# Perceiver block on one core: the latent projection one slot later, its z stores on ScalarE's queue, x1 stores and raw weight loads at the end of the stage

## The reference

```
x  = x + softmax(layernorm(x) @ ctx^T / sqrt(512), masked) @ ctx        # ctx: 256 rows per batch element
h  = layernorm(x)
q  = rmsnorm(h @ wq_a^T + b) @ wq_b^T + b ; kv, k_pe = split(h @ wkv_a^T + b) ; kv = rmsnorm(kv)
x  = x + causal latent attention (16 heads, rotary part of 64) @ wo^T + b
x  = layernorm(relu(x @ up)^2 @ down + (x @ expert) * top-2 gate sum) * gamma + beta
```

## Time and profile before

| | us |
|---|---|
| median of 3 runs | 1123.19 |
| lowest, highest | 1122.73, 1124.93 |
| the profiled execution | 1125.78 |
| its span | 1124.0 |
| PE busy in the span | 1093.4 (97%) |
| DVE, ACT, POOL busy | 532.3, 351.8, 322.5 |
| stage x and the seam end at about | 182 |

### The profile page before, as it was taken

How to read it: one execution, slowest core, us unless ns; L and a number is a source line. 1 busy time by engine, 2 the same in 40 slices (tenths; PEclk the granted TensorE clock), 3 DMA queues, 4 the chain that set the end, 5 groups by cost and what they waited for, 6 DMA issues and landing times.

```text
span 1124.0 us, 20917 instructions
## 1 busy us (share of the span) xinstructions
PE 1093.4 (97%) x8097; PEld 950.2 (85%) x8097; DVE 532.3 (47%) x998; ACT 351.8 (31%) x699; POOL 322.5 (29%) x370
## 2 busy tenths in 40 slices
PE   5999999999999999999999999999999999999996
PEld 2676686888888888888888888889899998989895
DVE  3565565534443444344443456746244443525242
ACT  4456554332322222222322225513121221213130
POOL 2343361121212111121112122525242332415151
PEclk9999999999999999999999999999999999999998
DMA  9999922002111111102111117401010010101000
GB/s 363 417 421 418 422 96 72 22 20 73 28 33 56 42 56 33 56 19 61 32 38 56 39 51 232 169 1 39 1 38 20 20 38 0 37 0 38 1 19 19
DMA packets 41279, 100.96 MB, mean 90 GB/s; under 512 B 7497, under 2 KB 11620, under 8 KB 36740
## 3 DMA queue, kind: packets, MB, share of 16 engines
q1 hardware_dynamic: 41220, 100.16, 24.8%
HBM read 74.45 MB, written 17.30 MB: 82 GB/s over the span
## 4 chain that ended last, share of the span: by engine, by line
PE 91%; DVE 2%; DMA 2%; issue 2%; POOL 1%; ACT 1%; SPq 1%; DVEq 0%; POOLq 0%
PE b_z L44 7%; PE b_z L45 6%; PE b_z L46 6%; PE b_score L44 5%; PE b_score L45 5%; PE b_score L46 5%; PE b_prob L44 5%; PE b_prob L46 5%; PE b_prob L45 5%; PE b_z L1095 3%; PE b_read L44 3%; PE b_free L44 2%; PE b_read L46 2%; PE b_read L45 2%; PE b_free L46 2%; PE b_free L45 2%
## 5 line engine op out<-in xcount | busy, mean ns | idle before, releaser
L811 POOL TENSOR_TENSOR m_e<-m_e,m_rs 128x512 f32<-128x512 f32 x32 | 34.7, 1085 | 357.3 <-DVE m_rs L966 357.3
L1441 POOL TENSOR_TENSOR f_hT_lo<-f_h,f_hT_hi 128x512 fp32r<-128x512 f32 x64 | 89.6, 1399 | 94.0 <-ACT f_hT_hi L1484 89.3
L46 PE MATMUL b_z<-m_zT_hi,m_wq_hi 128*128 128x256 f32 x384 | 108.7, 283 | 0.0
L44 PE MATMUL b_z<-m_zT_lo,m_wq_hi 128*128 128x256 f32 x384 | 108.7, 283 | 0.0
L45 PE MATMUL b_z<-m_zT_hi,m_wq_lo 128*128 128x256 f32 x384 | 108.7, 283 | 0.0
L1540 DVE TENSOR_TENSOR f_h<-f_h 128x512 f32<-128x512 f32 x64 | 70.6, 1104 | 61.5 <-ACT f_h L1479 61.5
L907 DVE TENSOR_TENSOR m_pT_lo<-b_turn,m_pT_hi 128x512 fp32r<-128x512 f32 x32 | 22.1, 692 | 160.3 <-ACT m_pT_hi L858 160.3
L852 ACT ACTIVATE m_qT<-b_z,m_q_bias 128x256 f32<-128x256 f32 x128 | 53.8, 472 | 79.1 <-PE b_z L46 75.3
L44 PEld LDWEIGHTS b_z<-m_zT_lo,m_wq_hi 128*128 128x128 f32 x384 | 73.7, 192 | 0.0
L45 PEld LDWEIGHTS b_z<-m_zT_hi,m_wq_lo 128*128 128x128 f32 x384 | 73.7, 192 | 0.0
L46 PEld LDWEIGHTS b_z<-m_zT_hi,m_wq_hi 128*128 128x128 f32 x384 | 73.7, 192 | 0.0
(11 more groups left out here) (226 smaller groups left out, 3189.6 us busy)
## 6 DMA issues: line engine op xcount, KB each, us to landing
x_ctx_in<-ctx_rows_dram SPq DMA_DIRECT2D x16, 1024.0 KB, 14.4
x_ctxT<-ctx_turned_dram SPq DMA_DIRECT2D x15, 1024.0 KB, 14.5
m_swapped<-m_by_sin SPq DMA_DIRECT2D x128, 64.0 KB, 2.0
z_scratch<-x_zbuf SPq DMA_DIRECT2D x16, 288.0 KB, 13.3
m_raw<-attn_raw_dram SPq DMA_DIRECT2D x6, 768.0 KB, 15.6
m_z_in<-z_scratch SPq DMA_DIRECT2D x8, 576.0 KB, 3.7
x_x_all<-x_dram SPq DMA_DIRECT2D x16, 256.0 KB, 14.8
x_scratch<-x_x_all SPq DMA_DIRECT2D x16, 256.0 KB, 14.8
```

Source lines behind the costliest of these rows:

```text
L44: nc.tensor.matmul(out, lh, rl, start=first, stop=False)
L46: return nc.tensor.matmul(out, lh, rh, start=False, stop=last)
L811: q.tensor_tensor(e[:], e[:], rs[:].unsqueeze(2).broadcast_to([P, HB, SEQ]), ALU.mult).then_inc(s["normed"], 1)
L1441: g.tensor_tensor(hT_lo[:, 2 * n:2 * n + 2].rearrange("p m n -> p (m n)"), h[:, n % 2], hT_hi[:, 2 * n:2 * n + 2].bitcast(F32).rearrange(" ...
```

## The change

The projection of pair p-2 in slot p becomes that of pair p-3, and everything behind it (bias, norm of z, its store) moves a slot too; the seam has one projection more, and pair 12's norm. The halves of the turned x1 get a second buffer. PE's order in a slot becomes score, read, turn1, turn0, project. The mask's product is the first of the scores instead of the last. w_hi is made by POOL in slot 2, behind `rstd_of(1, 1)`, and w_lo moves to the end of DVE's slot 2; w_raw is loaded behind x of pair 4. On DVE, `residual` moves ahead of `turned1_lo`; on ACT, `exp` and `scale_q` move ahead of `turned1_hi`. ACT issues the z stores at the end of its slot on its own queue (the last three stay SP's). SP stores x1 in three transfers: ten tiles in slot 13, five in slot 15, one in the seam. Keys are loaded in slot 10, the queries' pieces in slots 11, 12, 12, 13, 13 and 13, values in slot 14, the last piece in slot 15. The semaphores `x1_stored0` and `x1_stored1` become `x1_first` and `x1_rest`. The diff, cut:

```diff
-    xnT1_hi, xnT1_lo = pair("xnT1", [P, KH, P])
+    xnT1 = [pair("xnT1a", [P, KH, P]), pair("xnT1b", [P, KH, P])]
...
+    def write_z(eng, p, par):
+        eng.wait_ge(s["z_kv"], p + 1)
+        eng.wait_ge(s["z_rope"], p + 1)
+        eng.wait_ge(s["q_scaled"], p + 1)
+        eng.dma_start(z_t[p], zbuf[:, par]).then_inc(s[f"z_stored{par}"], 16)
...
-        def store_x1(p, par):
-            sp.wait_ge(s["x1_done"], p + 1)
-            if p >= 2:
-                sp.wait_ge(s[f"x1_stored{par}"], 8 * (p - par))
-            sp.dma_start(x1_t[p], x_all[:, p]).then_inc(s[f"x1_stored{par}"], 16)
+            write_z(sp, p, par)
+
+        def store_x1(first, n, done):
+            sp.wait_ge(s["x1_done"], first + n)
+            sp.dma_start(x1_t[first:first + n].rearrange("t p d -> p t d"), x_all[:, first:first + n]).then_inc(s[done], 16)
...
-            if p == KEYS_AT:
+            if p == 10:
                 w.load_keys(sp)
-            if p in QUERIES_AT:
-                w.load_queries(sp, QUERIES_AT.index(p))
+            for c in range(w.QUERY_LOADS):
+                if p == QUERIES_AT[c]:
+                    w.load_queries(sp, c)
             if p == PAIRS - 3:
+                store_x1(0, OVER_X, "x1_first")
+            if p == PAIRS - 2:
                 w.load_values(sp)
-            if has(p - 1):
-                store_x1(p - 1, 1 - par)
-            if p == PAIRS - 3:
-                for q in range(2):
-                    sp.wait_ge(s[f"x1_stored{q}"], 8 * OVER_X)
+            if p == PAIRS - 1:
+                sp.wait_ge(s["x1_first"], 16)
                 w.load_last(sp)
-            if has(p - 3):
-                store_z(p - 3, 1 - par)
+                store_x1(OVER_X, PAIRS - 1 - OVER_X, "x1_rest")
...
+        load_x(4)
         sp.dma_start(w_raw[:], A["w_latent"].rearrange("(k p) n -> p k n", p=P)).then_inc(s["w_loaded"], 16)
-        load_x(4)
...
-            if has(p - 3):
-                latent_rstd(p - 3)
-                rotate(p - 3, 1 - par)
+            if has(p - 4):
+                latent_rstd(p - 4)
+                rotate(p - 4, par)
             if has(p - 1):
                 rstd_of(1, p - 1)
+            if p == 2:
+                pool.wait_ge(s["w_loaded"], 16)
+                g.tensor_copy(w_hi[:], w_raw[:]).then_inc(s["w_hi"], 1)
...
-        def turned1_hi(p):
+        def turned1_hi(p, par):
             act.wait_ge(s["turned1"], p + 1)
-            act.wait_ge(s["z_made"], 2 * p)
-            a.copy(xnT1_hi[:].rearrange(flat), b_turn1[:]).then_inc(s["xT1_hi"], 1)
+            if not isinstance(p, int) or p >= 2:
+                act.wait_ge(s["z_made"], 2 * (p - 1))
+            a.copy(xnT1[par][0][:].rearrange(flat), b_turn1[:]).then_inc(s["xT1_hi"], 1)
...
-            if p == 2:
-                act.wait_ge(s["w_loaded"], 16)
-                a.copy(w_hi[:].rearrange(flat), w_raw[:].rearrange(flat)).then_inc(s["w_hi"], 1)
             if has(p + 1):
                 norm(0, p + 1, xn0, x_all[:, p + 1])
-            if has(p - 3):
-                squares(p - 3, 1 - par)
+            if has(p - 4):
+                squares(p - 4, par)
+            exp(p)
+            if has(p - 4):
+                scale_q(p - 4, par)
             if has(p - 2):
-                turned1_hi(p - 2)
-            exp(p)
-            if has(p - 3):
-                scale_q(p - 3, 1 - par)
+                turned1_hi(p - 2, par)
             if has(p + 1):
                 turned0(p + 1)
             if has(p - 1):
                 norm(1, p - 1, xn1, x_all[:, p - 1])
+            if has(p - 4):
+                write_z(act, p - 4, par)
...
         def slot(p, par):
             maximum(p)
+            if has(p + 2):
+                first_var(p + 2)
+            if has(p - 4):
+                latent_var(p - 4)
+            if has(p - 1):
+                residual(p - 1)
+            if has(p - 2):
+                turned1_lo(p - 2, par)
+            validate(p)
+            if has(p - 4):
+                latent_kv(p - 4, par)
+            if has(p - 3):
+                bias(p - 3, 1 - par)
+            if p == PAIRS - 3:
+                w.columns(dve)
             if p == 2:
                 dve.wait_ge(s["w_hi"], 1)
                 split(w_lo[:].rearrange(flat), w_raw[:].rearrange(flat), w_hi[:].rearrange(flat), s["w_lo"])
-            if has(p + 2):
-                first_var(p + 2)
-            if has(p - 3):
-                latent_var(p - 3)
-            if has(p - 2):
-                turned1_lo(p - 2)
-            if has(p - 1):
-                residual(p - 1)
-            validate(p)
-            if has(p - 3):
-                latent_kv(p - 3, 1 - par)
-            if has(p - 2):
-                bias(p - 2, par)
-            if p == PAIRS - 3:
-                w.columns(dve)
...
-        def project(p):
+        def project(p, par):
+            (xnT1_hi, xnT1_lo) = xnT1[par]
             pe.wait_ge(s["xT1_lo"], p + 1)
             if isinstance(p, int) and p == 0:
                 pe.wait_ge(s["w_lo"], 1)
...
+            if p == 0:
+                pe.wait_ge(s["masks_built"], 1)
+            t.matmul(b_score[:, 0:CTX], picks[:, p].bitcast(BF16), mask_rows, start=True, stop=False)
             for k in range(KH):
                 if p == 0 and k % 2 == 0:
                     pe.wait_ge(s[f"ctxT_first{k // 2}"], 16)
                 for b in range(2):
                     rows = slice(SEQ * b, SEQ * b + SEQ)
-                    t.matmul(b_score[rows, 0:CTX], xnT0[:, k, rows], ctxT[:, p % RING, k, CTX * b:CTX * b + CTX],
-                             start=k == 0, stop=False)
-            if p == 0:
-                pe.wait_ge(s["masks_built"], 1)
-            t.matmul(b_score[:, 0:CTX], picks[:, p].bitcast(BF16), mask_rows, start=False, stop=True).then_inc(s["scored"], 1)
+                    mm = t.matmul(b_score[rows, 0:CTX], xnT0[:, k, rows], ctxT[:, p % RING, k, CTX * b:CTX * b + CTX],
+                                  start=False, stop=k == KH - 1)
+            mm.then_inc(s["scored"], 1)
...
         def slot(p, par):
             score(p)
+            if has(p - 1):
+                read(p - 1)
             if has(p - 2):
                 turn1(p - 2)
-            if has(p - 1):
-                read(p - 1)
             if has(p + 1):
                 turn0(p + 1)
-            if has(p - 2):
-                project(p - 2)
+            if has(p - 3):
+                project(p - 3, 1 - par)
             pe.wait_ge(s["exped"], p + 1)
...
-            x["store_x1"](L, L % 2)
+            x["store_z"](L - 3, 1 - L % 2)
+            x["store_x1"](L, 1, "x1_rest")
             x["store_z"](L - 2, L % 2)
             X["tiles_stored"](sp)
...
             for n in range(weights.ROPE_ROUNDS):
                 w["rope_scaled"](n)
+            x["latent_rstd"](L - 3)
+            x["rotate"](L - 3, 1 - L % 2)
+            x["rstd_of"](1, L)
             x["latent_rstd"](L - 2)
-            x["rstd_of"](1, L)
             x["rotate"](L - 2, L % 2)
             w["rope_hi"](0)
             x["latent_rstd"](L - 1)
...
             x["turned_probs"](L)
-            x["turned1_hi"](L - 1)
+            x["squares"](L - 3, 1 - L % 2)
+            x["turned1_hi"](L - 1, 1 - L % 2)
+            x["scale_q"](L - 3, 1 - L % 2)
             w["keys_hi"](0)
             w["keys_hi"](1)
+            x["norm1"](L)
             x["squares"](L - 2, L % 2)
             x["scale_q"](L - 2, L % 2)
-            x["norm1"](L)
             w["keys_hi"](2)
-            x["turned1_hi"](L)
+            x["turned1_hi"](L, L % 2)
             w["keys_hi"](3)
             w["keys_hi"](4)
             x["squares"](L - 1, 1 - L % 2)
...
-            x["turned1_lo"](L - 1)
+            x["latent_var"](L - 3)
+            x["turned1_lo"](L - 1, 1 - L % 2)
+            x["latent_kv"](L - 3, 1 - L % 2)
+            x["bias"](L - 2, L % 2)
+            x["residual"](L)
             w["keys_lo"](0)
             w["keys_lo"](1)
             x["latent_var"](L - 2)
-            x["residual"](L)
             x["latent_kv"](L - 2, L % 2)
             x["bias"](L - 1, 1 - L % 2)
             w["keys_lo"](2)
-            x["turned1_lo"](L)
+            x["turned1_lo"](L, L % 2)
             w["keys_lo"](3)
             w["keys_lo"](4)
             x["latent_var"](L - 1)
...
             x["turn1"](L - 1)
+            x["project"](L - 2, L % 2)
+            x["read"](L)
             w["fill_keys"](0)
             w["fill_keys"](1)
-            x["read"](L)
-            x["project"](L - 1)
+            x["project"](L - 1, 1 - L % 2)
             w["fill_keys"](2)
             x["turn1"](L)
             w["fill_keys"](3)
             w["fill_keys"](4)
-            x["project"](L)
+            x["project"](L, L % 2)
             for f in range(5, weights.KEY_FILLS):
                 w["fill_keys"](f)
...
```

(15 more changed lines are left out.)

## The result

| us | before | after |
|---|---|---|
| median, 19 runs of each | 1124.72 | 1120.72 |
| ratio, 95% interval | | 0.9965 [0.9958, 0.9971] |
| the profiled execution, its span | 1125.78, 1124.0 | 1119.34, 1117.5 |
| start of slot 4 | 43.59 | 38.05 |
| start of slot 15 | 136.00 | 128.33 |

What follows compares the result with a forecast made beforehand. The prediction took PE (TensorE), not DMA, as the bound: -6.5 us at the start, 0 in the middle slots, +3.0 at the seam, net -3.5 against the median 1123.2, so 1119.7 us; range 1116.5 to 1125.0.

Steps and rivals of the forecast that it cites:

- step 4: Start: projection 0 waits 0.9 us instead of 2.94, at full clock; score 4 starts at 37.1 instead of 43.59, gain 6.5.
- step 1: Slot 0: the mask product now leads score 0 and waits for its operand, so all that follows is 0.9 us later.
- Steps 2 and 3: Slots 2 and 3: score 2 at 20.4; POOL casts w_hi in 2.2 us till 30.9; w_lo ends at 33.5.
- the slack of 1.3: Middle slots: the probabilities' copy ends 0.8 us into the slot, read comes at 2.1, leaving 1.3 us.
- PE's work is the same: Middle slots: they stay at 8.40 us each, with no gain or loss.
- Rival A: Slots 12 to 15: z stores stall ACT, costing 6.0 us together; +2.5 net, 1125.7 us; chance 0.14.
- Rival C: Start and seam: the mask wait and the seam wait are not seen; -6.1, 1117.1 us; chance 0.13.
- Rival D: Whole stage: DMA is the bound after all, so moving bytes later helps beyond PE's account; no size given; chance 0.03.
- The seam: From score 15 to the bias product: 33.7 us instead of 30.73, 3.0 longer, with one projection more.
- the 0.71: Seam: PE's earlier loss of 0.71 us goes, since lows 5 to 7 have 1.7 us more.
- the new wait: Seam: PE waits 1.7 us before projection 15, behind ACT's cast of turn 15; bounds 0 and 3.
- Rival B: Start: POOL's cast takes 4.1 us, PE waits 2.8, the clock falls, projection 0 costs +1.5; net -0.1, 1123.1; chance 0.2.

## Why the prediction was right, and where it was off

**The start** (step 4: score 4 at 37.1, gain 6.5) held. In the profiled execution it was 38.05, since step 1's 0.9 for the mask was 2.2 there; it is 1.2 in the mean, and over the six executions the start was 37.0. Steps 2 and 3 held in their lengths: w_hi 2.10 us (2.2 foreseen), at 29.79, w_lo till 34.49, both 1.0 to 1.1 later than foreseen, as score 2 (21.50 for 20.4) with the mask; projection 0 waited 0.62 (0.9) at full clock. A wait of 0.46 in slot 4 for the probabilities' copy was not foreseen: from slot 5 on no read waits, as the slack of 1.3 had it.

**The middle slots** are where the prediction failed: "PE's work is the same" was priced by the list of products and not by their order. They fell from 8.40 to 8.12, 2.1 us over eleven slots with slot 4's wait in it. The rows of before showed the four changes of width and no price for them; a range there should have reached below nothing.

**The z stores on ACT** (0.34 foreseen, 0.34 found) and **the late loads** (nothing) held, and the runs with each undone confirm that they are worth nothing. Rival A falls: all issues but the first took 0.34 us, and the longest landing was 10.3. Rival C falls, for both waits that it left out were seen. Rival D falls with full engines and slots of 8.12.

**The seam** came to 33.71 against 33.7, and that close is partly luck. The waits were 2.34 instead of 1.7: turn 14 waits 0.32 (foreseen 0), the 0.71 is gone, the new wait is 2.02 (1.7). PE's work was 31.37 instead of 31.94; two changes of width fewer, in slot 15, would be about half of that; the rest is not traced. The new wait stands behind ACT's cast as foreseen, since norm 15 came at 18.55 after the slot's start and POOL's scalings stood ahead of latent 12. That PE's wait was the last bound there was only half true: with fills moved into it, DVE's low halves were next.

**Rival B** (POOL's cast is slow and the gate falls) falls: the cast took 2.10 us, and the clock fell at the start in no profiled run of the changed kernel or its variants. It did fall in two seams (the mask last in every slot; z on SP), at 1.5 us, the price that B named.

Sum: -5.54 - 2.13 + 2.98 = -4.69 in the profiled execution, -4.0 in the medians, where -3.5 was foreseen; what failed was the sum's zero for the middle, partly set off by the mask. That the gain came within 0.5 us of the forecast is luck in part: the stretch behind the bias product, costed as a plain shift, differs by up to 3.4 us from execution to execution.

## What to carry to other kernels

Count, in PE's list, the changes between products of different array shapes, and put those of one shape together: here two changes fewer in a slot save 0.28 us of 8.40. Such an order needs room between a turn and its use; a lag of a slot gives it, and its price is paid once, at the seam, where it should be costed and refilled by hand. Look there for steps on VectorE with two SBUF operands beside long GpSimd steps: move them, not the work around them.

## What the runs showed of the hardware that was not expected

- A change between products of 128\*128 and 128\*64 costs PE 0.13 to 0.16 us here, without any idle time in its rows.
- A one-column GpSimd step took 2.56 us for 0.27 beside VectorE's split, and a VectorE step of 0.35 took 1.66, 2.00 and (in the kernel before) 3.00 beside GpSimd's split: the held step ended 0.1 to 0.2 us behind the other's end each time.
- ACT's DMA issue stays at 0.34 us while one instruction of SP's lasts 12.98.
- After a wait of 2.01 to 2.05 us at the same place, the clock stayed at 1.00 up to the bias product in five executions and fell in two (0.76 over 7 us in one).
- Behind the bias product the clock fell in twelve profiled executions of thirteen, and the same work took 15.7 or 17.4 us instead of 14.0.
